# Weighted values of two heads in one group of 32 partitions: one PSUM bank, one eviction and four transposes a batch instead of two, two and eight

## The reference, cut to what matters

```python
B, T, D, H = 16, 256, 128, 16          # head size HD = 8
# layer A, on the normalised x, causal
scores = einsum('bhqd,bhkd->bhqk', q, k) * HD ** -0.5
attn = softmax(scores + mask, axis=-1)
out = einsum('bhqk,bhkd->bhqd', attn, v).transpose(0, 2, 1, 3).reshape(b, t, d)
x = x + out @ wo + bo
x = x + ffn(layernorm(x))               # 8 experts, the best 2 for each token
# layer B: the same, not causal, with a score scale and a shift worked out for each head
x = x + weighted @ W_proj + b_proj
x = x + ffn(layernorm(x))
```

## Time and profile before

| | us |
|---|---|
| three runs | 1160.31, 1162.33, 1164.01 |
| median | 1162.33 |
| span of the profiled execution (no separate time is given for it) | 1164.9 |
| TensorE busy in the span | 1029.9 |
| VectorE, ScalarE, GpSimd busy | 755.5, 672.4, 525.5 |

### The profile page before, as it was taken

The page is one execution under the profiler, slowest core; times in us unless marked ns, Lnnn a source line. Parts: engine busy times, 40 slices in busy tenths (PEclk is TensorE's granted clock), DMA queues, the critical chain, the costliest instruction groups (busy, mean ns, idle before and its releaser), DMA issues.

```text
span 1164.9 us, 28879 instructions
## 1 busy us (share of the span) xinstructions
PE 1029.9 (88%) x9290; PEld 716.6 (62%) x9290; DVE 755.5 (65%) x2322; ACT 672.4 (58%) x1399; POOL 525.5 (45%) x980
## 2 busy tenths in 40 slices
PE   2998999897989999999798979999888799999990
PEld 1444555453468989999443434444443589999990
DVE  4687778877777333456777888888877663334442
ACT  2365676663644545556277858897757445455550
POOL 2243444332742610344687736455736436004455
PEclk9998999996989999999778979998888899999995
DMA  6446544562235878887544323343221469778873
GB/s 152 104 114 138 116 110 99 151 181 57 54 118 174 271 233 236 260 255 236 125 111 104 101 56 85 89 107 84 65 49 44 130 191 280 227 242 256 272 225 109
DMA packets 201723, 175.03 MB, mean 150 GB/s; under 512 B 19812, under 2 KB 160616, under 8 KB 201576
## 3 DMA queue, kind: packets, MB, share of 16 engines
q1 hardware_dynamic: 193384, 156.41, 49.1%
q0 software_dynamic: 8192, 16.79, 4.8%
HBM read 122.99 MB, written 50.14 MB: 149 GB/s over the span
## 4 chain that ended last, share of the span: by engine, by line
PE 60%; DVE 11%; issue 6%; POOL 5%; DMA 4%; SPq 3%; ACT 1%; POOLq 0%; ACTq 0%; DVEq 0%
PE psS L1358 9%; PE psT L1365 9%; PE psO L321 8%; PE psS L355 7%; PE psO L1381 4%; PE psN L1381 4%; DVE mx L671 4%; PE psS L386 3%; PE psT L363 3%; POOL xn L1259 3%; PE psM L276 2%; PE psN L328 2%; DMA eo<-ysb 2%; PE psN L337 1%; PE psM L1346 1%
## 5 line engine op out<-in xcount | busy, mean ns | idle before, releaser
L671 DVE TENSOR_REDUCE mx<-psS 128x3 f32<-128x384 f32 (+1 forms) x512 | 311.4, 617 | 119.5 <-PE psS L386 61.8
L355 PE MATMUL psS<-kst,qst 48*128 48x256 bf16 (+1 forms) x1024 | 201.7, 286 | 46.4 <-DVE mx L671 33.2
L558 ACT ACTIVATE pT<-psT,scb 128x512 f32<-128x512 f32 x256 | 193.9, 777 | 43.2 <-PE psT L363 40.7
L363 PE MATMUL psT<-qst,kst 50*128 50x256 bf16 (+1 forms) x1024 | 194.7, 278 | 4.6 <-DMA qst<-scr_m 2.2
L1422 DVE TENSOR_TENSOR hT<-sg,psT 128x512 f32<-128x512 f32 x142 | 97.5, 686 | 154.4 <-PE psT L1365 127.7
L1245 POOL DMA_INDIRECT xg<-xn,slot x128 | 123.1, 962 | 131.3 <-DVE ysb L1417 72.1
L1358 PE MATMUL psS<-xTt,wgc 128*128 128x128 f32 x1136 | 153.7, 279 | 5.7 <-issue 5.3
L355 PEld LDWEIGHTS psS<-kst,qst 48*128 48x128 bf16 x1024 | 66.2, 97 | 146.0 <-DVE mx L671 68.2
L1365 PE MATMUL psT<-xTt,wuc 128*128 128x128 f32 x1136 | 152.2, 278 | 1.5 <-DMA wuc<-in_L_ffn_Wu 1.4
L790 POOL TENSOR_SCALAR_AFFINE_SELECT pT<-pT 128x256 f32<-128x256 f32 x224 | 90.6, 412 | 133.0 <-ACT pT L553 131.8
L553 ACT ACTIVATE pT<-psT 128x384 f32<-128x384 f32 x256 | 122.9, 490 | 46.1 <-PE psT L363 35.9
(11 more groups left out here) (225 smaller groups left out, 1595.1 us busy)
## 6 DMA issues: line engine op xcount, KB each, us to landing
wgc<-in_L_ffn_Wg SPq DMA_DIRECT2D x142, 256.0 KB, 3.1
wuc<-in_L_ffn_Wu SPq DMA_DIRECT2D x142, 256.0 KB
scr_part<-part SPq DMA_DIRECT2D x128, 128.0 KB, 2.1
qst<-scr_part SPq DMA_DIRECT2D x64, 192.0 KB, 3.7
kst<-scr_part SPq DMA_DIRECT2D x64, 192.0 KB, 4.7
xin<-xg SPq DMA_DIRECT2D x142, 64.0 KB
eo<-ysb SPq DMA_DIRECT2D x142, 64.0 KB
scr_part<-part SPq DMA_DIRECT2D x32, 192.0 KB, 1.9
```

The lines of the kernel that those rows point to most:

```text
L355: return nc.tensor.matmul(ps[:, c0:c0 + n], q_[r64, t, q0], k_[r64, t, 0:n], start=(half == 0), stop=True, skip_group_check=True)
L363: return nc.tensor.matmul(ps[:, c0:c0 + T - q0], k_[m64, t, half * P:half * P + P], q_[m64, t, q0:T], start=(half == 0 or not L.causal), s ...
L558: nc.scalar.activation(pT[:, g % 8, 0:cols], psT[g % 2][:, 0:cols], ACT.Exp, scale=scb[r][:, 0, i:i + 1], bias=scb[r][:, 1, i:i + 1]).then ...
L671: nc.vector.tensor_reduce(mx3[:, u, 0:n, pos:pos + 1].rearrange("p a b -> p (a b)"), psS[h % 2][:, 0:kcols(L)].rearrange("p (a k) -> p a k ...
```

## The change

The values of head h now stand at columns 16 to 23 of its 32 in `vp`, the 1 at column 24. Quads 2 and 3 read the 32 columns of their heads as they are, so that their results land in rows 16 to 24 of each group of 32 partitions. Quads 0 and 1 read 32 columns from column 16 on (their own values first, then the zeros at the start of the next head's), so that theirs land in rows 0 to 8. All four quads add into one bank, `psO[0]`: the first product of quad 0 clears it, all others accumulate. One eviction, at h = 2 of the next step, replaces two; `oT` is half as large; `out_transposes` has two products where it had four, at the same two places. `normalise` reads the same number of elements out of `psN` with another stride, and writes them to the same places of `on`. The waits on the `oT` semaphore count one eviction a batch; two of the router's waits on it are dropped, and the ones at h = 3 of step 19 now wait for the eviction at h = 2.

```diff
-        vp = [sb(f"vp{r}", [P, 2, H, 32]) for r in range(RING)]
+        vp = [sb(f"vp{r}", [P, 2, H * 32 + 16]) for r in range(RING)]
-        oT = sb("oT", [P, 4, T])
+        oT = sb("oT", [P, 2, T])
...
-                if q % 2 == 0:
-                    after(pe, s["oT"], 2 * (b - 1) + q // 2 + 1)
+                if q == 0:
+                    after(pe, s["oT"], b)
+                pair, region = q // 2, q % 2
...
-                        o0 = (q % 2) * T
-                        last = nc.tensor.matmul(psO[q // 2][32 * i:32 * i + 32, o0 + dst[0]:o0 + dst[1]],
-                                                vp[r][:, kb, h, :], pT[:, h % 8, src[0]:src[1]],
-                                                start=(kb == 0), stop=(kb == 1), skip_group_check=True)
+                        o0, v0 = region * T, 32 * h + 16 * (1 - pair)
+                        last = nc.tensor.matmul(psO[0][32 * i:32 * i + 32, o0 + dst[0]:o0 + dst[1]],
+                                                vp[r][:, kb, v0:v0 + 32], pT[:, h % 8, src[0]:src[1]],
+                                                start=(q == 0 and kb == 0), stop=(pair == 1 and kb == 1),
+                                                skip_group_check=True)
...
             def out_transposes(qb):
-                for q in range(4):
+                for q in range(2):
                     last = nc.tensor.transpose(psN[:, q * P:(q + 1) * P], oT[:, q, qb * P:(qb + 1) * P], ident[:])
...
-            def evac_oT(b, half):
-                after(act, s["PV"], 4 * b + 2 * half + 2)
+            def evac_oT(b):
+                after(act, s["PV"], 4 * b + 4)
                 after(act, s["tO_ps"], 2 * b)
-                nc.scalar.activation(oT[:, 2 * half:2 * half + 2, :], psO[half][:].rearrange("p (a t) -> p a t", a=2),
+                nc.scalar.activation(oT[:], psO[0][:].rearrange("p (a t) -> p a t", a=2),
                                      ACT.Copy).then_inc(s["oT"], 1)
...
-                if h == 13 and T_:
-                    evac_oT(bT, 0)
...
-                o4 = psN[:].rearrange("p (h c) -> p h c", c=32)
-                nc.vector.reciprocal(rden[:], o4[:, :, HD]).then_inc(s["rden"], 1)
+                o4 = psN[:, 0:2 * P].rearrange("p (m a c) -> p m a c", a=2, c=2 * HD)
+                den = rden[:].rearrange("p (m a) -> p m a", a=2)
+                nc.vector.reciprocal(den, o4[:, :, :, HD]).then_inc(s["rden"], 1)
...
                 if j == 19 and h in (3, 6, 9):
                     if h == 3:
-                        pe.wait_ge(L.s["oT"], 2 * B - 1)
+                        pe.wait_ge(L.s["oT"], B)
```

More of the change, by code:

```diff
@@ L243, in build, with heads_of @@
         LB.s["pT"] = LB.s["exp"]
+        def heads_of(v):
+            return v[:, :, 0:32 * H].rearrange("p k (h c) -> p k h c", c=32)
         def kcols(L):
@@ L433, in pe_step @@
                 if h == 4 and O_:
-                    after(pe, s["oT"], 2 * bO + 2)
+                    after(pe, s["oT"], bO + 1)
                     if T_:
@@ L534, in act_step @@
                 if h == 2 and O_:
-                    evac_oT(bO, 1)
+                    evac_oT(bO)
                 if h == (3 if L.causal else 4) and P_:
@@ L639, in normalise @@
                 after(dve, s["onT_ps"], 2 * bO + qb)
-                o4 = psN[:].rearrange("p (h c) -> p h c", c=32)
-                nc.vector.reciprocal(rden[:], o4[:, :, HD]).then_inc(s["rden"], 1)
+                o4 = psN[:, 0:2 * P].rearrange("p (m a c) -> p m a c", a=2, c=2 * HD)
+                den = rden[:].rearrange("p (m a) -> p m a", a=2)
+                nc.vector.reciprocal(den, o4[:, :, :, HD]).then_inc(s["rden"], 1)
                 after(dve, s["rden"], 2 * bO + qb + 1)
-                nc.vector.tensor_tensor(out=on[:].rearrange("p (h c) -> p h c", c=HD), in0=o4[:, :, 0:HD],
-                                        in1=rden[:].unsqueeze(2).to_broadcast([P, H, HD]),
+                nc.vector.tensor_tensor(out=on[:].rearrange("p (a m c) -> p m a c", a=2, c=HD), in0=o4[:, :, :, 0:HD],
+                                        in1=den.unsqueeze(3).to_broadcast([P, 8, 2, HD]),
                                         op=ALU.mult).then_inc(s["on"], 1)
@@ L705, in dve_step @@
                         ins = nc.vector.tensor_tensor(
-                            out=vp[rS][:, k, :, 0:HD], in0=psM[:, k * P:(k + 1) * P].rearrange("p (h c) -> p h c", c=HD),
+                            out=heads_of(vp[rS])[:, k, :, 16:16 + HD], in0=psM[:, k * P:(k + 1) * P].rearrange("p (h c) -> p h c", c=HD),
                             in1=L.b_wide[:, 0, :].rearrange("p (h c) -> p h c", c=HD), op=ALU.add)
@@ L775, in pool_step @@
                     for r in range(RING):
-                        nc.gpsimd.memset(vp[r][:, :, :, HD:HD + 1], 1.0).then_inc(s_mset, 1)
+                        nc.gpsimd.memset(heads_of(vp[r])[:, :, :, 16 + HD:17 + HD], 1.0).then_inc(s_mset, 1)
             if not L.causal and 0 <= j - 1 < B:
@@ L991, in pe_route @@
             if k == ROUTE_T:
-                pe.wait_ge((LA, LB)[l].s["oT"], 2 * B)
+                pe.wait_ge((LA, LB)[l].s["oT"], B)
                 pe_tokens(pe, n, QUADS[1] - 1)
@@ L1570, in hook @@
                     if h == 6:
-                        pe.wait_ge(L.s["oT"], 2 * (j - 4) + 2)
                         for i in range(2):
```

## The result

| | before | after |
|---|---|---|
| runs, us | 1160.31, 1162.33, 1163.0, 1164.01 | 1169.19, 1169.52, 1170.24, 1172.75 |
| median | 1162.66 | 1169.88 |
| ratio, 95% interval | | 1.0068 [1.005, 1.0087] |
| span of the profiled execution | 1164.9 | 1171.0 |
| mean granted clock of the profiled execution | 0.920 | 0.900 |

The change made the kernel slower by 0.7%, 7 us; 5.3 us faster was forecast. The profiled execution of the changed kernel is the slowest of its four runs, at the lowest clock of them (0.900; the others 0.906 to 0.909).
The page of the changed kernel first: its span, and the chain that ended last by line, whose row answers to the earlier trace rows. L334 is now the transposes (L328 before), L326 the value products, L361 the score products.

A forecast was written before the change was run, and what follows sets the result against it. TensorE was taken to hold almost all of both layers' step periods, with gains limited by its neighbours' slack. The terms 2.0 + 1.0 + 1.0 + 0.6 + 0.7 gave 5.3 us, so 1157.0 us; range 1150 to 1162.5.

The forecast's parts named there:

- The plain steps: Steps repeating with one period: 0.25 us each in layer A, 2.0 in all; 0.14 each in B, 1.0 in all.
- new wait: Layer A, before the transpose of `on` at h = 13: about 0.14 us of waiting for VectorE.
- the half (0.09): Layer B plain steps: without the eviction, half of the projection weight load's 0.18 us wait is gained, 0.09.
- The two waits named as signs: Layer B: a wait for the reduction before h = 5's product; h = 12's transposed-score product 0.06 us behind its exponential.
- The uneven steps of layer A: One transpose group each in j = 14, 15, 16 and both of j = 17: 5 x 0.2 = 1.0 us gained.
- the end of layer A: Transposes of j = 18 and 19 are on the chain: 0.7 us gained before GpSimd's last scatter takes over.
- the uneven steps of layer B: One transpose group in j = 16 (0.2 us) and the half-clock group at 881.61 (0.4): 0.6 us gained.
- Rival C: Slower through the clock: value-product groups falling to 1.2 GHz cost 0.86 us each; at 14 groups, 1169 us. Chance 0.10.
- the sentence that the 1.00 gives no sign of a fall: The granted clock of 1.00 in the steps shown gives no sign that less TensorE work could cost time.
- rival A: It all counts: every transpose place gives its 0.21 us, 13.7 us in all, 1148.6 us. Chance 0.12.

The follow-up runs named there:

- g2: Kernel before, with only two of the four oT transposes in steps 17 to 19 of layer B: 1164.08 us, ratio 0.9997.
- i4: Kernel before, both banks and evictions kept, with only two of four oT transposes at every place of layer B: 1165.65 us, ratio 1.001.
- e3: Changed kernel with a second 128 x 512 ScalarE copy at h = 13, where the removed eviction stood: 1166.62 us, ratio 1.0011.
- g4: Changed kernel with two idle transposes more at each place of layer A alone: 1172.05 us, ratio 1.0067.
- r_after: The changed kernel itself, run again among the experiments: 1169.76 us, ratio 1.0034 to the kernel before.
- h1: Changed kernel with two idle transposes more in layer B at h = 11 alone: 1163.68 us, ratio 1.0014.
- h2: h1 with eight idle products in step 18 of layer B as well: 1163.84 us, ratio 1.0007.
- h4: Changed kernel with eighty idle products in steps of both layers and two idle transposes at h = 11 of layer B: 1166.97 us, ratio 1.0023.

## Why the prediction was wrong

**The plain steps** were right. Layer A: 15.88 to 15.63, 8 x 0.25 = 2.0 as summed. `on` is ready at 159.47 + 0.29 = 159.76 and its transpose starts 0.05 behind, at 159.81. The value products ahead of it start at 158.92, 0.89 earlier, where before the distance was 161.82 - 161.03 = 0.79: 0.10 of new wait for the 0.14 that was forecast (VectorE's row, then TensorE's):

```profile
159.47 0.29 DVE L648 TENSOR_TENSOR on<-psN,rden 128x128 f32<-128x128 f32 x1
```

```profile
159.81 0.33 PE L339 MATMUL psN<-ident,on 128*128 128x128 f32 x1
```

Layer B: 17.54 to 17.45, 0.09 a step against 0.14. The runs split it: 17.50 with both evictions and two transposes gives the transposes 0.04 (forecast 0.05); from there to 17.45 the eviction is worth 0.05, below the half (0.09) that I took of its wait but within its ends of 0 and 0.18. `onT` does start at once behind its transpose (ScalarE, against the earlier trace rows), and the weight load of the projection no longer waits. The two waits named as signs are there as well: in B11 the score product of h = 5 starts 0.06 behind its reduction (748.39, 748.33), the transposed-score product of h = 12 0.06 behind its exponential (756.21, 756.15).

```profile
758.96 0.28 ACT L535 ACTIVATE onT<-psN 128x128 f32<-128x128 f32 x1
```

```profile
759.50 0.41 PEld L343 LDWEIGHTS psN<-w_inB,onT 128*128 128x128 f32 x2
```

**The uneven steps of layer A** came out in sum: j = 14 to 17 gave 0.25 + 0.26 + 0.06 + 0.44 = 1.01 us for 1.0. That it fits to a hundredth is luck: j = 16 gave 0.06 of its 0.2, and j = 15 had 3.1 us more at the low clock. Of the end of layer A, 0.23 of 0.7 shows in A18; the rest lies in a stretch (A19 to B4) whose low-clock time differs between executions, 272.11 us after with 37.5 low against 276.03 with 44.4, and can't be read.

**The step that failed** is the 0.6 us gain of the uneven steps of layer B, and beneath it what the whole sum rests on without saying so: that each stretch keeps the granted clock that it had before. B16 to B18 lost 10.4 us (71.2 for 60.8) in the profile and 9.2 in the second. Where the clock is the same, the gain is there: in g2, with two transposes in these steps, B17 takes 16.52 us for the 16.85 of before, both at 0.86, which is 0.33 of the 0.4 forecast for that step, and B18 13.04 for 13.26, both at 1.00:

```profile
878.83:895.35 16.52, 14.98 (x138) 6.22 (x137) 12.59 (x33) 13.58 (x23) 12.55 (x14) 0.86 0.17 54
895.35:908.39 13.04, 11.64 (x114) 5.81 (x113) 11.52 (x58) 11.25 (x19) 9.99 (x11) 1.00 0.16 53
```

**Rival C** named the mechanism. That its 1169 is the time that came is luck, as its working was off in three places. It priced a fall at 0.86 a group of value products: that was right for the group (0.85), but the projection behind it falls too, 1.64 a step. It looked for it in the plain steps, where it came 11 times in 10 profiles, 1.8 us an execution, far from the 14 groups that it needed. The larger part came in the last steps of layer B, which I had read for the order of work and not for the clock: there B16 and B17 have 0.74 and 0.86 before the change, so that stretch hung by a margin that the 1.00 of the earlier trace rows said nothing of. And the sentence that the 1.00 gives no sign of a fall was the error of judgement: a granted clock of 1.00 shows on which side of the edge a step stands, not how near. The Trainium skill (TensorE: Matmul & The Clock Gate, "What's actually happening") has the throttled state as the default which activity releases; the trace agrees in the direction (less TensorE work, mean clock 0.909 for 0.921), and I gave it 0.10. (One slip in the range: 1150 is not half of the way from 1157.0 to rival A's 1148.6 but 0.83 of it.)

**What stays open.** The falls in plain steps (1.8 us) and two long stays of 9 to 10 us in ten profiles are together near 4 us an execution, where layer B loses 6 to 8 us against four transposes. Both long stays are in profiles of the changed kernel itself. Each kernel has one profile or two, of one execution; where the clock was low in the others isn't recorded. Nor is it settled what starts the long stay: idle products in step 18 end it (B18 14.18), and so, in their profiles, do a second copy on ScalarE and four transposes in layer A (60.8), which leave layer B's late TensorE work as it is. That speaks for theory 2's kind of cause, the position of the stretches, beside theory 3's, and so does B7. By the time, i4 (only the transposes taken out of layer B, ratio 1.001) and e3 (only the eviction's place filled again, 1.0011) lie under g4's 1.0067 but not clear of r_after's 1.0034, so what share the transposes have and what share the eviction isn't settled. That idle work in layer B gives the time back is shown; how it does so in each stretch is not.

## What to carry to other kernels

Where TensorE is busy for over 90% of a step, taking work from it can cost more than it gives: before counting on such a cut, read the granted clock of every stretch, the uneven ones first, and price each that shows less than 1.00 at both levels. If the cut loses, put idle products back where they lie beside a wait and time again; here one product of 512 columns at each place of layer B (0.2 us) was worth 6 to 8 us. Take ten runs with their clocks, not three: runs of one kernel show by their spread what the clock does to it. Between kernels the mean clock alone tells little, since idle work raises it too.

## What the runs showed of the hardware

- A fall in the plain steps of layer B began each time 0.85 to 1.11 us after the start of the same instructions (the h = 4 transposes), in eight kernels and different steps, with no wait of TensorE over 0.23 us in the 3 us ahead of it and TensorE busy for 16.5 of 17.45 us in such a step. It came in seven of seven profiles with two transposes there and a B7 under 28.2 us and in none of three with four; idle transposes at h = 11 don't keep it away (h1, h2, h4). For an idle product at that place no profile shows it.
- Four transposes are no protection elsewhere: in g4, step 9 of layer A took 17.89 us for 15.88, with the clock low from 165.13, 0.77 us after TensorE had waited 0.94 us for a DMA.
- TensorE can stay at 1.2 GHz while it is busy 20.07 of 20.40 us.
- More clock isn't more speed: eighty idle products raised the mean clock from 0.909 to 0.927, the highest here, and the time was no better than with eight.
